# Routing computed in one batch behind the layernorm, with its indexed writes early, and the steps of the last layer rearranged

## The reference

```
xn = layernorm(x)                                     # layer 0
s  = attention(xn)      # 2 query heads, one k and v, rope, causal softmax, Wo
f  = sum over the 2 best of 8 experts of prob * ((gelu(xn Wg + bg) * (xn W1 + b1)) W2 + b2)
x  = x + s * silu(f)
xn = layernorm(x)                                     # layer 1
h  = rmsnorm(xn); local = causal conv of h, 7 taps
decay = clip(sigmoid(h Wdecay + b), .05, .95); gate = sigmoid(h Wgate + b)
state = cumsum(gate*h / max(cumprod(decay) shifted, 1e-7)) * cumprod(decay) * scale
mixed = xn + concat(local, state, mem(h)) Wc + bc
s  = mixed + (silu(h2 Wg) * (h2 Wup)) Wdown,          h2 = rmsnorm(mixed)
x  = x + s * silu(tanh(xn W a1 a2 + bias))
```

## Time and profile before

| | |
|---|---|
| three runs | 624.75, 629.97, 628.24 us, median 628.24 |
| profiled execution | 624.81 us, its span 622.5 us |
| mean granted TensorE clock | 0.944 |
| TensorE, VectorE, ScalarE, POOL busy | 88%, 65%, 42%, 40% |
| first indexed write into `slots_x` starts | 66.8 us |
| first expert transpose | 181.4 us |
| first rows of the last layer added on POOL | 400.6 us |

### The profile page before, as it was taken

The page is one execution under the profiler, slowest core; times in us unless marked ns, Lnnn a source line. Parts: engine busy times, 40 slices in busy tenths (PEclk is TensorE's granted clock), DMA queues, the critical chain, the costliest instruction groups (busy, mean ns, idle before and its releaser), DMA issues.

```text
span 622.5 us, 13285 instructions
## 1 busy us (share of the span) xinstructions
PE 549.4 (88%) x3235; PEld 406.1 (65%) x3236; DVE 405.1 (65%) x1181; ACT 258.5 (42%) x743; POOL 246.2 (40%) x420
## 2 busy tenths in 40 slices
PE   7987899999949999999999998547988988979986
PEld 4845566676639999999999997433443443543542
DVE  6879887777705556555565555366778867777723
ACT  4333546455424554545555454422331422422411
POOL 6300356656623444444444444252424335244100
PEclk9669999999959999999999999858999999999989
DMA  9990452111117788888887881900000000000000
GB/s 293 218 190 19 152 188 93 55 58 44 39 35 220 240 235 235 239 229 242 230 238 230 232 239 48 263 0 0 0 18 0 17 17 0 17 17 0 17 17 17
DMA packets 54458, 72.29 MB, mean 116 GB/s; under 512 B 6288, under 2 KB 41136, under 8 KB 54176
## 3 DMA queue, kind: packets, MB, share of 16 engines
q1 hardware_dynamic: 39888, 58.35, 34.5%
q0 software_dynamic: 4320, 8.92, 4.3%
q10 hardware_dynamic: 10224, 4.73, 2.7%
HBM read 54.15 MB, written 15.74 MB: 112 GB/s over the span
## 4 chain that ended last, share of the span: by engine, by line
PE 46%; DVE 11%; issue 7%; POOL 4%; SPq 2%; DMA 1%; ACT 1%; DVEq 0%; ACTq 0%; POOLq 0%
PE bank L770 10%; PE bank L778 10%; PE bank L787 10%; SPq L424 2%; PE bank L896 2%; PE bank L853 2%; PE bank L902 2%; DVE W1E L1291 1%; DVE SPARE L1232 1%; PE bank L846 1%; DVE X L1210 1%; POOL SPARE L544 1%; PE bank L762 1%; PE bank L847 1%; PE bank L881 1%
## 5 line engine op out<-in xcount | busy, mean ns | idle before, releaser
L1170 DVE SCALAR_TENSOR_TENSOR AR<-bank,B1T,AR 128x128 f32<-128x128 f32 x284 | 80.1, 345 | 72.0 <-ACT AR L1498 61.4
L1498 ACT ACTIVATE AR<-bank,BGT 128x128 f32<-128x128 f32 x284 | 81.2, 368 | 59.0 <-PE bank L770 55.8
L515 POOL DMA_INDIRECT rows_y<-YO,DST x71 | 69.7, 982 | 79.6 <-DVE YO L1154 70.7
L471 POOL DMA_INDIRECT slots_x<-XR,SLOT x64 | 62.6, 979 | 88.5 <-DVE TEXP L1065 44.2
L770 PE MATMUL bank<-AR,WGE 128*128 128x128 f32 x568 | 76.6, 279 | 0.2 <-ACT AR L1491 0.2
L778 PE MATMUL bank<-AR,WGE 128*128 128x128 f32 x568 | 75.9, 277 | 0.0
L787 PE MATMUL bank<-W2E,AR 128*128 x568 | 75.3, 276 | 0.5 <-DVE AR L1170 0.5
L770 PEld LDWEIGHTS bank<-AR,WGE 128*128 128x128 f32 x568 | 70.5, 195 | 0.6 <-issue 0.6
L778 PEld LDWEIGHTS bank<-AR,WGE 128*128 128x128 f32 x568 | 70.0, 194 | 0.0
L787 PEld LDWEIGHTS bank<-W2E,AR 128*128 128x128 f32 x568 | 69.1, 192 | 1.0 <-issue 0.9
L1413 ACT ACTIVATE AR<-bank,AR 128x512 f32<-128x512 f32 (+1 forms) x64 | 33.9, 530 | 66.7 <-DVE AR L1099 66.7
(11 more groups left out here) (184 smaller groups left out, 979.5 us busy)
## 6 DMA issues: line engine op xcount, KB each, us to landing
WGE<-in_wgu SPq DMA_DIRECT2D x71, 512.0 KB, 4.6
XG<-slots_x ACTq DMA_DIRECT2D x71, 65.0 KB, 4.1
slots_x<-W1E SPq DMA_DIRECT2D x7, 585.0 KB, 13.5
X<-in_x SPq DMA_DIRECT2D x8, 256.0 KB, 5.1
AR<-XNT SPq DMA_DIRECT2D x8, 256.0 KB, 4.0
W2E<-in_w SPq DMA_DIRECT2D x1, 2048.0 KB, 9.2
XR<-rows_y SPq DMA_DIRECT2D x8, 256.0 KB, 4.6
XNT<-rows_y SPq DMA_DIRECT2D x8, 256.0 KB, 5.4
```

The lines of the kernel that those rows point to most:

```text
L471: pool.indirect_dma_start(out=slots_x, out_offset=bass.IndirectOffsetOnAxis(ap=SLOT[:, k, n:n + 1], axis=0), in_=XR[:, n, :], in_offset=No ...
L515: pool.indirect_dma_start(out=rows_y, out_offset=bass.IndirectOffsetOnAxis(ap=DST[q][:, 0:1], axis=0), in_=YO[q % 2][:], in_offset=None).t ...
L1170: s = dve.scalar_tensor_tensor(out=HT[u][:, c, :], in0=B[3 + u][:, c * P:(c + 1) * P], scalar=B1T[:, bass.ds(e, 1), c], in1=ZB[u][:, c, :] ...
L1498: act.activation(ZB[u][:, c, :], B[1 + u][:, c * P:(c + 1) * P], ACT.Gelu, bias=BGT[:, bass.ds(e, 1), c]).then_inc(c_gelu, 1)
```

## The change

**Layernorm.** VectorE makes `VE` (in `stats`) and `NMR` (`spread`); POOL keeps only the pow. `project` of batches 0 and 1 reads `XNT` directly, and SP no longer stages them. SP issues the zero fill of `slots_x` first, then the stages of batches 2 and 3, the weights, and, after the new semaphore `r_texp`, the first experts.

**Routing.** `top_two` becomes `logits` and `choose`, which finds the best expert of all 32 tiles by five instructions of 128x256, and again after masking the first choice. Parts 0, 2, 3, 4 and 1 stand before the first attention round, part 5 behind its third row maximum. `count` writes bank 2 and stands before the fourth projection of batch 0. `SLOT` raises `r_slot` itself; `TEXP` raises `r_texp`.

```
-            top_two(0)
+            logits(0)
...
-            for part in range(3):
-                rope(0, 0, part)
-            top_two(1)
+            rope(0, 0, 0)
+            logits(1)
+            route(0)
+            rope(0, 0, 1)
+            route(2)
+            route(3)
+            route(4)
+            route(1)
+            rope(0, 0, 2)
             attend(0, 0, first=True)
...
+            def choose(k, lg):
+                iexn = CST[:, None, C_EXN:C_EXN + E].broadcast_to([P, NT, E])
+                link(dve.tensor_reduce(TOP[:, k, :], lg, AX.X, ALU.max))
+                link(dve.tensor_tensor(HIT, lg, TOP[:, k, :, None].broadcast_to([P, NT, E]), ALU.is_equal))
+                link(dve.tensor_tensor(HIT, HIT, iexn, ALU.mult))
+                link(dve.tensor_reduce(IXF[:, k, :], HIT, AX.X, ALU.min))
+                link(dve.tensor_tensor(by_expert(OH[:, k, :]), iexn, IXF[:, k, :, None].broadcast_to([P, NT, E]),
+                                       ALU.is_equal))
...
                 if part == 0:
+                    dve.wait_ge(r_lg, 2)
+                    choose(0, LG)
+                    link(dve.scalar_tensor_tensor(out=LG2, in0=by_expert(OH[:, 0, :]), scalar=BELOW, in1=LG,
+                                                  op0=ALU.mult, op1=ALU.add))
+                    choose(1, LG2)
                     dve.tensor_tensor(MB, OH[:, 0, :], OH[:, 1, :], ALU.add).then_inc(r_m, 1)
```

On TensorE and ScalarE, before the first round:

```
             for step in range(3):
                 composite(step)
-                if step == 1:
-                    pe.wait_ge(cvo_done, 1)
-                    project(0, 0, 3)
+            count()
+            project(0, 0, 3)
...
+            act.wait_ge(r_cnt, 1)
+            act.activation(CNT.rearrange("p a b -> p (a b)"), B[2][:], ACT.Copy).then_inc(r_cnt_out, 1)
+            act.wait_ge(r_sh, 1)
+            act.activation(SH, SH, ACT.Exp)
+            act.activation(DIF, DIF, ACT.Exp).then_inc(r_exp, 1)
             values(0, 0)
```

**Last layer.** VectorE's orders in a step:

```
                 if not last:
                     d_local(b + 1, 1)
                     d_local(b + 1, 2)
-                    d_decay(b + 1)
                 d_h2_of(b)
                 if not last:
+                    d_decay(b + 1)
                     d_cumulate(b + 1)
+                if front:
+                    d_later_stats(b + 2)
                 d_gated(b, 0)
+                if front:
+                    d_aggregate(b + 2)
                 if not last:
-                    d_update(b + 1)
+                    d_floor(b + 1)
                 d_gated(b, 1)
-                if front:
-                    d_front2(b + 2)
                 if not last:
                     d_local(b + 1, 3)
-                    d_scan(b + 1)
                 d_gated(b, 2)
                 d_gated(b, 3)
+                if not last:
+                    d_scan(b + 1)
                 if front:
                     d_front3(b + 2)
                 d_sum(b)
```

```
             for b in range(NSEQ):
                 rms(b)
                 if b + 2 < NSEQ:
                     front(b + 2)
+                    add_x(b + 2)
                 if b + 1 < NSEQ:
+                    update_gated(b + 1)
                     update(b + 1)
                 if b + 2 < NSEQ:
                     scales(b + 2)
+                gate_out(b)
...
+            def d_scaled(b):
+                act.wait_ge(d_xn, b + 1)
+                act.wait_ge(d_r, b + 1)
+                for i in range(TPS):
+                    s = act.activation(HS1[:, i, :], XN1[:, i, :], ACT.Copy, scale=R2[:, i:i + 1])
+                s.then_inc(d_hs, 1)
...
+                act.wait_ge(d_td, b + 1)
+                act.activation(DEC, DEC, ACT.Copy, bias=0.5, scale=0.5).then_inc(d_da, 1)
+                act.wait_ge(d_tg, b + 1)
+                act.activation(GTE, GTE, ACT.Copy, bias=1.0).then_inc(d_gp, 1)
```

More of the change, by code:

```diff
@@ L277, in build @@
         r_slot = sem("r_slot")
+        r_texp = sem("r_texp")
         zero_set = sem("zero_set")
@@ L372, in _ @@
                 sp.dma_start(slots_x_t[:, tiles, :], ZERO[:, 0:tiles.stop - tiles.start, :]).then_inc(zero_out, 16)
+            for b in range(2, 4):
+                sp.wait_ge(a_xnt, b + 1)
+                stage(b, b % 2)
             sp.dma_start(BGT[:], t["bg"]).then_inc(ld_moe, 16)
@@ L385, in load_expert @@
                 sp.dma_start(WB[:, q:q + 1, :], t["wgu"][:, bass.ds(e, 1), :]).then_inc(w_ld[q], 16)
-            for b in range(2, 6):
+            sp.wait_ge(r_texp, 1)
+            sp.wait_ge(zero_out, 16 * 8)
+            for j in range(WBUFS):
+                load_expert(j, j)
+            sp.wait_ge(a_xnt, NSEQ)
+            for b in range(4, 6):
                 sp.wait_ge(proj_full, 4 * (b - 1))
-                if b == 2:
-                    sp.wait_ge(a_xnt, NSEQ)
                 stage(b, b % 2)
[L392 to L396, removed]
                 if b == 4:
@@ L574, in _ @@
             scales(1)
+            update_gated(0)
             update(0)
@@ L705, in attend @@
                         weigh(b if k >= 2 else b - 1, u if k >= 2 else 1 - u, (k - 2) % NS)
-                    if first and k == 2 and isinstance(b, int) and b == 0:
-                        count()
             def finish(b):
@@ L1001, in by_expert, with logits @@
                 return v.rearrange("p (n e) -> p n e", e=E)
-            def top_two(half):
+            def logits(half):
                 dve.wait_ge(a_lg, NSEQ // 2 * (half + 1))
@@ L1116, in attend @@
                         rope(b + 1, 1 - u, (k - 1) // 2)
-                    if isinstance(b, int) and b == 0:
-                        for part in ROUTE_AFTER[k]:
-                            route(part)
+                    if isinstance(b, int) and b == 0 and k == 2:
+                        route(5)
                     if last:
@@ L1262, in d_mixed @@
             def d_mixed(b):
+                if not (isinstance(b, int) and b == 0):
+                    dve.wait_ge(d_s, b)
                 dve.wait_ge(d_comb, b + 1)
@@ L1598, in d_step @@
                     d_turned(b + 1)
-                if not last:
                     d_local0(b + 1)
-                    d_gates(b + 1)
                 d_gate1(b)
@@ L1604, in d_step @@
                     d_xturned(b + 1)
-                d_silu(b, 0)
                 if front:
                     d_front2(b + 2)
+                if not last:
+                    d_gates(b + 1)
+                d_silu(b, 0)
                 d_silu(b, 1)
@@ L1611, in d_step @@
                 d_silu(b, 3)
+                if front:
+                    d_scaled(b + 2)
             act.wait_ge(c_ht, SLOT_TILES)
```

196 lines of the change are left out of this document (108 added, 88 removed).

## The result

The changed kernel takes 607.46 us (median of 4 runs, 606.28 to 608.54) against 629.11 us (4 runs, 624.75 to 634.52): ratio 0.966, interval [0.962, 0.970]. It was timed twice more, each time beside the kernel before on one chip: 606.71 us, 0.976 [0.971, 0.980], and 605.89 us, 0.972 [0.967, 0.976]. Medians here are over all runs of a kernel, while ratios and intervals leave out those that fell into a slower state of the chip. So the gain is 17 to 22 us, where 10.8 was forecast. The profiled execution has a span of 604.3 us against 622.5: 18.2 less.

What follows compares the result with a forecast made beforehand. TensorE, busy 88% of the span, was taken as the bound, its idle and slow-clock time as what could be won. Early routing +1.7 and last layer -12.5 make -10.8 us, from 628.24 to 617, range 607 to 626.

Steps and rivals of the forecast that it cites:

- Attention's delay: Early routing and layernorm: first row maximum 15.1 us later, 3.7 given back in the first round, attention 11.4 us late.
- 17.35 + 0.9 + 2.0 = 20.3: First attention round: a plain round's 17.35 us, plus 0.9 for routing part 5 and 2.0 for the slow clock.
- The seam: Between attention and experts: writes no longer last, ScalarE 4.5 us later, full clock for first tiles; early routing nets +1.7 us.
- The last layer: Work leaves VectorE and waits go: step 24.41 to 22.2 us in about five steps, with entry and last steps -12.5 us.
- new wait at the first product: Last layer, each step: the first down-projection waits about 0.8 us because cumulate and statistics moved.
- the 0.4 left for the transposes: Last layer, each step: of TensorE's 1.35 us wait for transposes, 0.4 us was to remain.
- The entry: Start of the last layer: first transposes need one pow and four scalings less but a ScalarE pass more, gaining 2 us.
- The last step: End of the last layer: the last two steps lose 0.5 us, the product with `G1` costing 1.27 on POOL for 0.69.
- the signs: What would show it in the last layer: `X` stored every 22.2 us, VectorE below 14 us a step, POOL at 13.
- Rival 3: Last layer: VectorE and POOL excluding each other on SBUF ports replaces the removed work, kernel slower at 638 us; chance 0.09.
- Rival 1: First rounds swallow attention's delay, or the last layer reaches TensorE's floor: about -7 more, 606 to 611 us; chance 0.22.
- Rivals 2 and 4: 2: POOL's queue halves the last-layer gain, 624 us, chance 0.18; 4: stretched slot writes stay last, some 622, chance 0.06.

Runs made afterwards that it cites:

- a0: The changed kernel again, timed beside the kernel before on a second chip: 606.71 us, ratio 0.976.
- f1: Changed kernel with the last layer's gated output, gated update and addition to `X` back on VectorE: 606.45 us, 0.976 of the kernel before.
- f2: Changed kernel with the last layer's four scalings of `HS1` back on VectorE: 611.20 us, 0.983 of the kernel before.
- g0: The changed kernel again, timed beside the kernel before on a third chip: 605.89 us, ratio 0.972.
- e1: Kernel before with only the layernorm and routing part of the change, last layer as before: 631.91 us, 1.002 of the kernel before.
- g2: Changed kernel with gated output, gated update, addition to `X` and scalings of `HS1` back on VectorE: 605.33 us, 0.971 of the kernel before.
- g1: Kernel before with only the rearranged last layer, routing as before, on the third chip: 605.80 us, 0.971 of the kernel before.
- g3: Changed kernel, third rotation before routing steps, three of these inside the first attention round, four extra TensorE products before the projection: 603.71 us, 0.963 of before.
- e3: Changed kernel with POOL's indexed writes held back until the first attention round's exponentials are done: 614.75 us, 0.979 of the kernel before.
- e4: Changed kernel with batch 0's third rope ahead of routing parts 2, 3, 4 and 1: 610.44 us, 0.972 of the kernel before.
- f3: Changed kernel with seven extra TensorE products between the counts and the value projection: 606.65 us, 0.979 of the kernel before.

## Why the prediction was right, and where it was not

The forecast had the sign and both places; its size was half to two thirds of what came. 607.46 us is at the lower edge of the range (607 to 626), the two later medians are just below it.

- **Attention's delay, 11.4 us forecast, 7.2 measured in the first pair of profiles, 10.4 on the average of ten.** The way to the first row maximum was right (56.2 or 57 forecast, 55.72; `route(0)` ended at 38.5 for 37.8; the projection took 3.78 for 3.75; the first write started at 49.71 for 48.8, the last had landed by 162.8 for 159). The step that failed is "17.35 + 0.9 + 2.0 = 20.3" for the first round: it is 17.35. The clock was up at 54.9, before the first maximum, 4.1 us after TensorE took up work; I had taken the 9.1 us of the kernel before, another execution's history. Part 5 hid itself. That the average delay is still near 11.4 is luck: the 2.8 us that the first round is shorter are largely made up by first maxima that lie 16.9 us apart on average, for 15.1.
- **The seam, +1.7 forecast, -4.4 in the first pair, about 0 over the runs.** The mechanism is as forecast in its first half: the writes stop being last, and attention is last. The clock did not always stay up: in a0, f1 and f2 it was 0.50 for 3.4 us of the first tiles, in the changed kernel's first profile, g0, e1 and g2 it was not. With a delay of 7.2 instead of 11.4 the sum would have been -2.5. The first transpose came at 179.49, not at 184 to 186. But by the runs (e1 1.002; g1 level with g0) and by the average of the profiles the part is worth no more than I said, with either sign. The clock at the start differs between executions by as much as this part moves: the second round of the seven profiles starts anywhere from 72.9 to 77.9.
- **The last layer, -12.5 forecast, -15.2 in the profile; this is the term that was mis-sized.** The step was said to fall by 2.2 to 22.2 and fell by 3.07 to 21.34, close to the floor of TensorE, "21.2". The 0.8 of a new wait at the first product is 0.3, the 0.4 left for the transposes hides beside other work, TensorE's 0.9 of weight-load wait at the roots (L577's pow, held to 1.58 us) was not forecast and costs nothing visible either. The entry gave 3.2 for 2. The last step cost 1.8 more in the profile, for 0.5: its clock was at 0.50 for 6.8 us (3.4 in the kernel before); in g3's profile it was not at all, and that step was 18.77 us, 2.9 less. Of the signs, POOL came out at 12.45 us a step for 13, VectorE at 14.80, not below 14.
- **The reason given for it was mostly wrong, so that the sum came near is partly luck.** I priced 5.3 us of work taken off VectorE; 3.90 came off its busy time. g2 puts 2.35 us of that back and loses 0.47. The gain is in what g2 keeps, the order above all by the traces, and I had treated the order as a source of new waits: I named the transposes' wait of 1.35 us, but not VectorE's own 2.31 us for POOL ahead of it. Which of the reorderings gives how much of the 2.60 us was not tried one by one; that the earlier statistics are the larger part is read from the traces, not isolated.
- **Rival 3, the ports.** The meetings are there: in the changed kernel the cumulative product takes 2.00 us beside POOL, and 1.23 in g2 where POOL is idle; the clamp 0.96 and 0.43. But they fall in VectorE's slack: the step is 21.34 us all the same. The sum of this rival was wrong as well: 13.4, five times 1.0 and 8.7 make 27.1, not 25.7, and its threshold was then 2.3 us held, not 3.7. These are the rows of the changed kernel:

```profile
498.53 0.96 DVE L1294 TENSOR_SCALAR WGE<-WGE 128x512 f32<-128x512 f32 x1
499.53 2.00 DVE L1298 TENSOR_TENSOR_SCAN W2E<-WGE,SPARE 128x512 f32<-128x512 f32 x1
```

- **Rival 1** gave 606 to 611 with 0.22 and its second half is what happened: the last layer came down to TensorE's floor. It should have had more of the chance: a step had 3.2 us of idle TensorE to give, and both waits of the earlier trace rows lost what stood ahead of them. The bound for that case was also added up too low: five steps of 3.2 us with the entry and the last steps are -17.5, not -16. **Rivals 2 and 4** are ruled out by the step, 21.34 for 23.3 to 23.7, and by the writes, which end 13 us before they are wanted.

## What to carry to other kernels

Before pricing the work that leaves an engine, look for that engine's own waits in the step: an idle VectorE ahead of a late result is a sign that the order is at fault, and here moving work off it won little. Two waits that end at the same place (here the writes and attention) must be moved together: advancing one by delaying the other was worth nothing. Where executions of one kernel differ by 5 us with the granted clock, a single profile settles a mechanism, never a gain of 4 us; and two profiles are best compared when their clock took the same course up to the place in question.

## What the runs showed of the hardware

- The granted clock of the same code differs between executions. It was 0.50 from 14 to 26 us in all fourteen profiles, with TensorE recorded as busy throughout. In nine of them it came up between 26 and 40 us; in five (e1, e3, e4, g2, g3) it was still 0.50 at 40. In g2 the first row maximum then came at 59.9, and at 55.6 in g0, whose code is the same up to there.
- After the idle stretch ahead of attention the clock rose 2.9 to 5.8 us after work resumed in the seven profiles with the changed start, 9.1 us after in the kernel before. In f3 it held at 1.00 over 4.6 us of idleness and fell 0.8 us into the work that followed.
- Instructions hold each other on VectorE and POOL also where one is small: the pow on 4 elements a partition took 1.58 us beside VectorE's multiply-add of two inputs (L1333) and 1.02 without it in g2; a 4-element addition took 1.70 beside two VectorE instructions in a row (before) and 0.67 beside the end of one (g2). VectorE's clamp between two constants (L1294, one input from SBUF), 0.43 in g2 without POOL, took 0.96 beside it.
